# Moving one operand of the wide VectorE operations from SBUF to PSUM in a four-layer graph network

## The reference, cut to what matters

```python
x = layernorm(x + L0(x))   # two hops of a normalised, weighted neighbour sum, relu, times W0, plus b
x = layernorm(x + L1(x))   # attention, 8 heads of 32; the edge's term is relu(edge_attr3 @ encW + b)
x = layernorm(x + L2(x))   # attention, 8 heads of 32; the edge's term is edge_attr64 @ W_e @ attn_e
x = layernorm(x + L3(x))   # filter network on the edges, message x[col] * filt, sum by row, MLP, batch norm

# attention (L1 and L2 alike):
ex  = exp(alpha - segment_max(alpha, dst)[dst])
out = segment_sum(h[src] * ex / segment_sum(ex, dst)[dst], dst) + bias
# filter:
filt = silu(rbf @ Wf1 + bf1) @ Wf2 + bf2
agg  = segment_sum(x[col] * filt, row)
```

## Time and profile before

| | |
|---|---|
| median of 3 runs | 8960.01 us (8955.36 to 8965.5) |
| the profiled execution | 8954.23 us, span 8952.5 us |
| busy share of the span | PE 53%, DVE 70%, ACT 37%, POOL 62% |
| mean granted TensorE clock | 0.721 |
| attention 1 | about 2859 to 4010 us |
| nodes 1 | about 4030 to 4680 us |
| attention 2 | about 4695 to 5735 us |
| nodes 2 | about 5745 to 6335 us |
| filter | about 6340 to 7706 us |

### The profile page before, as it was taken

How to read it: one execution, slowest core, us unless ns; L and a number is a source line. 1 busy time by engine, 2 the same in 40 slices (tenths; PEclk the granted TensorE clock), 3 DMA queues, 4 the chain that set the end, 5 groups by cost and what they waited for, 6 DMA issues and landing times. The chain is left out here.

```text
span 8952.5 us, 103278 instructions
## 1 busy us (share of the span) xinstructions
PE 4724.6 (53%) x18908; PEld 3435.4 (38%) x18908; DVE 6238.9 (70%) x20123; ACT 3276.4 (37%) x8442; POOL 5545.9 (62%) x5121
## 2 busy tenths in 40 slices
PE   8855000019998333337771111100588888799944
PEld 4422000018886211225551111100455555688833
DVE  7899333348887999988987777799544444455577
ACT  4533001337776111117870000144322222244499
POOL 7877777765554666657767777677788888300000
PEclk9999555559998555559995555555677777899955
DMA  0299899989997444549994444599544444566699
GB/s 21 82 345 345 287 304 301 308 281 303 303 302 235 147 146 148 147 133 313 337 310 119 122 123 122 156 273 269 130 79 79 79 79 79 131 202 202 192 342 345
DMA packets 1143019, 1839.84 MB, mean 206 GB/s; under 512 B 218094, under 2 KB 564898, under 8 KB 1142374
## 3 DMA queue, kind: packets, MB, share of 16 engines
q1 hardware_dynamic: 637094, 927.78, 31.4%
q0 software_dynamic: 257536, 587.44, 25.7%
q10 hardware_dynamic: 247744, 318.00, 10.4%
HBM read 1044.55 MB, written 788.03 MB: 205 GB/s over the span
## 5 line engine op out<-in xcount | busy, mean ns | idle before, releaser
L701 POOL DMA_INDIRECT st<-S,last_i x1176 | 1421.0, 1208 | 650.3 <-issue 316.4
L915 POOL DMA_INDIRECT rows<-T,src_i x784 | 802.6, 1024 | 251.0 <-issue 248.6
L642 ACT ACTIVATE xo<-z,shift,rsd 128x256 f32<-128x256 f32 x1568 | 854.7, 597 | 4.4 <-issue 4.4
L1128 POOL DMA_INDIRECT A<-comb,ai x392 | 702.6, 1792 | 159.2 <-issue 143.9
L931 PE MATMUL psE<-encs,attr 4*128 4x256 f32 x784 | 404.8, 668 | 743.3 <-DMA attr<-in_attr3T 743.3
L946 ACT ACTIVATE ex<-diff 128x32 f32<-128x32 f32 x392 | 89.9, 229 | 1711.7 <-DVE diff L993 1711.7
L1200 DVE TENSOR_SCALAR eq<-psI,src_f 128x128 f32<-128x128 f32 x392 | 136.8, 349 | 742.6 <-DMA A<-comb,ai 708.7
L931 PE MATMUL psE<-fes,attr 64*128 64x8 f32 x784 | 199.5, 363 | 823.0 <-DMA attr<-in_attr64T 820.7
L477 DVE SCALAR_TENSOR_TENSOR sums<-sums,same,rows 128x256 f32<-128x256 f32 x784 | 380.7, 486 | 322.3 <-ACT rows L458 308.0
L1142 PE MATMUL psH<-rbf,wf1s 20*128 20x256 f32 x784 | 279.9, 486 | 600.2 <-DMA rbf<-in_rbfT 600.2
L931 PEld LDWEIGHTS psE<-encs,attr 4*128 4x128 f32 x784 | 227.4, 319 | 920.4 <-DMA attr<-in_attr3T 882.7
(11 more groups left out here) (232 smaller groups left out, 15603.8 us busy)
## 6 DMA issues: line engine op xcount, KB each, us to landing
X<-xo ACTq DMA_DIRECT2D x588, 256.0 KB
xt<-X SPq DMA_DIRECT2D x588, 256.0 KB
S<-sums SPq DMA_DIRECT2D x392, 272.0 KB, 2.4
A<-zero SPq DMA_DIRECT2D x392, 256.0 KB, 4.7
S<-sums SPq DMA_DIRECT2D x392, 256.0 KB, 4.1
xt<-in_x SPq DMA_DIRECT2D x392, 256.0 KB
T<-tt ACTq DMA_DIRECT2D x196, 280.0 KB
T<-tt ACTq DMA_DIRECT2D x196, 272.0 KB
```

The source lines that it names most:

```text
L642: ins = e.activation(y[s][:, k, :], z[s][:, k, :], ACT.Identity, bias=shift[s][:, k, :], scale=rsd[s][:, k, :])
L701: e.indirect_dma_start(st[s][:, k, :], None, sums_table, bass.IndirectOffsetOnAxis(ap=last_i[:, c:c + 1], axis=0))\
L915: e.indirect_dma_start(rows[s][:, k, :], None, table, bass.IndirectOffsetOnAxis(ap=src_i[:, c:c + 1], axis=0))\
L1128: e.indirect_dma_start(A[k], bass.IndirectOffsetOnAxis(ap=ai[s][:, k, :], axis=0), comb[s][:, k, :], None, compute_op=ALU.add).then_inc(si ...
```

## The change

In five stages one operand of each wide VectorE operation that had two SBUF inputs is placed in PSUM.

- **nodes 1 and 2**: the bias is copied once into the bank `psBias`; the denominators `den` lie in a bank `psDen`; `mix` writes its product into one of two banks `psMix` in place of `z`, and `add` reads it there. `mix` waits for the `add` of two steps back, and the wait for the old `z` moves to `add`.
- **attention 1 and 2**: the exponentials `ex` lie in two banks `psX`, so ScalarE's exponential waits for the `add` of two steps back where it waited for that of four steps back. The rescaled sum goes to a bank `psD` and is read there by the addition.
- **attention 1**: ScalarE rectifies in place in `psE`, and VectorE's product reads `psE` and still writes `enc`. TensorE's `encode` waits for `scored` of two steps back, where it waited for `rectified`.
- **filter**: the bias is added in place in `psF`, and the product reads `psF`.

No operation is added in a step and none is taken away; one copy of 128x256 is added ahead of each of the two node stages.

```diff
@@ layer_nodes @@
-                den = tiles("den", H) if layer else None
...
+                if layer:
+                    psBias, psDen, psMix = bank("psBias", D), bank("psDen", NS * G * H), [bank(f"psMix{j}", G * D) for j in range(2)]
+                    den = [psDen[:, s * G * H:(s + 1) * G * H].rearrange("p (g h) -> p g h", g=G) for s in range(NS)]
...
                         bias = (b0s, b1s, b2s)[layer]
+                        if layer:
+                            e.tensor_copy(psBias[:], bias[:]).then_inc(spread_bias, 1)
+                            e.wait_ge(spread_bias, 1)
+                            bias = psBias
...
-                                ins = e.tensor_scalar(den[s][:], v[:, :, :, HD], 1e-10, None, ALU.max)
+                                ins = e.tensor_scalar(den[s], v[:, :, :, HD], 1e-10, None, ALU.max)
...
-                            e.reciprocal(den[s][:], den[s][:]).then_inc(signal(st_["weighed"], s), 1)
+                            e.reciprocal(den[s], den[s]).then_inc(signal(st_["weighed"], s), 1)
...
-                            hold(e, *done(st_["normed"], i, s, NS))
+                            hold(e, *done(st_["summed"], i, s, 2))
                             v = st[s][:, :, 0:VW].rearrange("p g (h w) -> p g h w", h=H)
-                            e.tensor_tensor(z[s][:].rearrange("p g (h d) -> p g h d", h=H), v[:, :, :, 0:HD],
-                                            den[s][:].rearrange("p g (h w) -> p g h w", w=1).to_broadcast([P, G, H, HD]), ALU.mult)\
+                            e.tensor_tensor(psMix[s % 2][:].rearrange("p (g h d) -> p g h d", g=G, h=H), v[:, :, :, 0:HD],
+                                            den[s].rearrange("p g (h w) -> p g h w", w=1).to_broadcast([P, G, H, HD]), ALU.mult)\
                                 .then_inc(signal(st_["mixed"], s), 1)
...
+                                hold(e, *done(st_["normed"], i, s, NS))
                                 hold(e, *done(st_["mixed"], i, s))
-                                more = z[s][:]
+                                more = psMix[s % 2][:].rearrange("p (g d) -> p g d", g=G)
@@ attention_edges @@
+                psX = [ctx.enter_context(psum(f"psX{j}", [P, 512], F32)) for j in range(2)]
+                ex = [psX[s % 2][:, 0:G * 2 * H].rearrange("p (g h) -> p g h", g=G) for s in range(NS)]
+                psD = ctx.enter_context(psum("psD", [P, 512], F32))
...
-                            if layer == 1:
-                                hold(e, *done(rectified, i, s, 2))
-                            else:
-                                hold(e, *done(scored, i, s, 2))
+                            hold(e, *done(scored, i, s, 2))
...
-                            hold(e, *done(scored, i, s, NS))
-                            e.activation(enc[s][:].rearrange("p g d -> p (g d)"), psE[s % 2][:], ACT.Relu).then_inc(signal(rectified, s), 1)
+                            e.activation(psE[s % 2][:], psE[s % 2][:], ACT.Relu).then_inc(signal(rectified, s), 1)
...
-                            hold(e, *done(summed, i, s, NS))
-                            e.activation(ex[s][:], diff[s][:], ACT.Exp).then_inc(signal(exped, s), 1)
+                            hold(e, *done(summed, i, s, 2))
+                            e.activation(ex[s], diff[s][:], ACT.Exp).then_inc(signal(exped, s), 1)
...
-                                link(e.tensor_tensor(e4, e4, hd, ALU.mult))
+                                r4 = psE[s % 2][:].rearrange("p (g h d) -> p g h d", g=G, h=H)
+                                link(e.tensor_tensor(e4, r4, hd, ALU.mult))
...
-                                e.tensor_tensor(heads(sums[s][:, k, 0:VW]), heads(last), r, ALU.mult).then_inc(bsteps, 1)
+                                e.tensor_tensor(heads(psD[:, 0:VW]), heads(last), r, ALU.mult).then_inc(bsteps, 1)
                                 e.wait_ge(bsteps, i * (NS * B) + (s * B + n))
-                                ins = e.tensor_tensor(sums[s][:, k, 0:VW], sums[s][:, k, 0:VW], rows[s][:, k, 0:VW], ALU.add)
+                                ins = e.tensor_tensor(sums[s][:, k, 0:VW], psD[:, 0:VW], rows[s][:, k, 0:VW], ALU.add)
@@ filter_edges @@
-                            e.tensor_tensor(fl[s][:], psF[s % 2][:].rearrange("p (g d) -> p g d", g=G),
-                                            bf2s[:].rearrange("p (g d) -> p g d", g=1).to_broadcast([P, G, D]), ALU.add).then_inc(msteps, 1)
+                            filt = psF[s % 2][:].rearrange("p (g d) -> p g d", g=G)
+                            e.tensor_tensor(filt, filt, bf2s[:].rearrange("p (g d) -> p g d", g=1).to_broadcast([P, G, D]), ALU.add).then_inc(msteps, 1)
                             e.wait_ge(msteps, i * NS + (s + 1))
-                            e.tensor_tensor(fl[s][:], fl[s][:], rows[s][:], ALU.mult).then_inc(signal(message, s), 1)
+                            e.tensor_tensor(fl[s][:], filt, rows[s][:], ALU.mult).then_inc(signal(message, s), 1)
```

More of the change, by code:

```diff
@@ L673, in layer_nodes @@
                 stored_t = stage_of("stored_t", NS, 1 + layer % 2)
-                ones = semaphore("ones")
+                ones, spread_bias = semaphore("ones"), semaphore("spread_bias")
                 TURN, PRODUCT, ADD = 1, 2, 3 if layer == 0 else 1
@@ L879, in attention_edges @@
                 enc = tiles("enc", D) if layer == 1 else None
-                lg, dot, mp, diff, ex = tiles("lg", H), tiles("dot", H), tiles("mp", H), tiles("diff", 2 * H), tiles("ex", 2 * H)
+                lg, dot, mp, diff = tiles("lg", H), tiles("dot", H), tiles("mp", H), tiles("diff", 2 * H)
+                psX = [ctx.enter_context(psum(f"psX{j}", [P, 512], F32)) for j in range(2)]
+                ex = [psX[s % 2][:, 0:G * 2 * H].rearrange("p (g h) -> p g h", g=G) for s in range(NS)]
+                psD = ctx.enter_context(psum("psD", [P, 512], F32))
                 EW = D if layer == 1 else H
```

## The result

The changed kernel takes 8829.6 us in the median of 4 runs (8827.0 to 8831.6), the kernel before 8962.8 us in the median of its 4. The ratio is 0.9851, with a 95% interval of 0.984 to 0.9863. The two profiled executions are 8954.2 and 8827.0 us, 127 us apart. The forecast was 8840.

A forecast was written before the change was run, and what follows sets the result against it. GpSimd was taken to bound the filter and attention 2, VectorE nodes 2 and attention 1, the `psV` loop nodes 1. -71 - 36 - 8 - 5 + 0 = -120 us, from 8960 to 8840 us; range 8800 to 8925.

The forecast's parts named there:

- My 5 us for nodes 1: Nodes 1: GpSimd and VectorE get slack, the `psV` loop stays; step 3.25 to 3.22 us or so, -5 us.
- my idea of it: Gathers and scatters: GpSimd waits with reading row numbers until VectorE's second SBUF read is over; filter scatter 1.98 against 1.62 us.
- Filter -71: Filter: GpSimd sets the pace; the scatter of 1.98 us falls to 1.62, step 6.94 to 6.58 us, -71 us.
- attention 2 -36: Attention 2: GpSimd never rests; four gathers per step fall to 0.946 us each, step 5.18 to 5.0 us, -36 us.
- nodes 2 -8: Nodes 2: VectorE stays at 2.91 us per step, so only stalls go, 2.95 to 2.91, -8 us.
- attention 1's 0: Attention 1: GpSimd is not the limit in VectorE's chain, so shorter gathers give 0.
- what is late next: Attention 1: if a moved wait is not passed already, the `rectified` tile is late, 15 us per 1000 at stake.
- bounds of -25 and +74: VectorE's write to PSUM, in no row: cost bounded by -25 and +74 ns per operation, taken as 0.
- The rival's count of four operations in nodes 2: Dearer PSUM operands: L712, L736, L750, L763 each pay in nodes 2, six operations in attention 1; chance 0.16.
- one sign of being wrong: Signs against: L1008 or L1010 grow, a landing gap opens before the filter's first scatter, or its scatter stays at 1.98.
- The waits that the change moved: Waits of `mix`, `add`, the exponential and `encode`: each is passed already, cost 0.

The follow-up runs named there:

- two_sbuf_ahead: Changed kernel plus an unused 128x512 addition with two SBUF operands between the filter's two multiply operations; 8883.8 us in one run.
- one_sbuf_ahead: Changed kernel plus two unused 128x256 statistics operations, one SBUF operand each, between the filter's two multiply operations; 8845.1 us in one run.
- more_two_sbuf: Kernel before plus an unused 128x512 addition with two SBUF operands right behind the filter's product L1220; 8974.8 us in one run.

## Why the prediction was right

*Which engine sets each stage.* Right as far as the runs go. GpSimd in the filter and attention 2, VectorE in nodes 2, the loop through `psV` in nodes 1, VectorE's chain in attention 1. In nodes 1 the gathers are shorter by 23% (376 to 291 us of 500) and the stage by 0.4 us. That its loop through `psV` is the limit is read from the waits; no run changes that loop. My 5 us for nodes 1 were the difference of a mean and one pair of rows, and nothing stood behind them.

*A second SBUF read under way holds a gather or scatter back.* Right, and shown by the pair `two_sbuf_ahead` and `one_sbuf_ahead`: +0.27 us for a scatter, against nothing. One part of my idea of it, which the sum did not use, was wrong: back-to-back operations let GpSimd in between (`more_two_sbuf`). That is not always so. Of 34 gathers of the node stages before that began in the first of two such operations back to back, 11 waited until 0.557 us after the second one's start as well, and the longest gather took 1.957 us. What decides is open.

In the words of the Trainium skill, "SBUF — State Buffer", section "Who interferes with whom", a VectorE instruction with two SBUF inputs contends with a GpSimd instruction that reads SBUF. The trace agrees, 1.98 us against 1.59. The section's remark that `tensor_tensor` was not seen to stall DMA does not hold for these indirect DMAs, by the same two numbers.

*The sizes.* Filter -71 against -69, attention 2 -36 against -36, nodes 2 -8 against -8.5. That the whole fits as well as its parts (-120 against -123) is luck in part: attention 1 gave 9 us more than forecast, and nodes 1 nearly 5 less.

*The term that was mis-sized is attention 1's 0.* It is -9.2 us, -10.1 in the run with the attention stages alone, and -11.6 in the means of five executions. I had the row: the wait for the rectified tile, 15 us in 1000, and called it what is late next, never what might go. It fell to 5.5, and 9 us less per 1000 are about 11 over the stage's 1170. Which edit did it isn't told apart: ScalarE's two operations of a step became shorter with their output in PSUM (597 to 582 ns and 229 to 201), the in-place tile changed the waits of `encode`, and the gathers, which share the DMA engines with the load of `attr`, became shorter.

*The price of a PSUM operand on VectorE.* I took 0 with bounds of -25 and +74. Wide operations changed by -7 to +11 ns: in attention 1 the weighting of the rows 703 to 696, the rescaled sum (now from SBUF and PSUM into PSUM) 427 to 433, the addition 433 to 432; in nodes 2 `mix` 683 to 692; the filter's bias addition 684 to 695. The small ones of nodes 2 took more, the clamp (L731 before) 148 to 167 and the reciprocal (L736 before) 231 to 249. The rival's count of four operations in nodes 2 left out the clamp, which writes `psDen` too. The step of nodes 2, where each would have counted, went from 2.908 to 2.904 us in the median. By the letter one sign of being wrong came, the rescaled sum grew; but by 6 ns, and the median step of attention 1 is the same. "VectorE: DVE Perf Modes" of the Trainium skill, section on the TRN2 errata, has 62 cycles more for a source in PSUM. No row here shows them, in an isolated chain or back to back.

*The waits that the change moved* show up in no row of VectorE. In the two attention stages and the two node stages of the changed kernel it waits for what it waited for before, the rectified tile, ScalarE's `sd` and the gathered rows, and for 3 us of 850 for `psE` in attention 2, where `encode` waits as it did.

## What to carry to other kernels

When GpSimd issues indirect DMAs without a rest and they take longer than their minimum (here 945 ns), look at what VectorE runs when they start. If it is an operation with two SBUF inputs, one of them can be had from PSUM, for wide operations at a price of 11 ns or less here. The gain is the lengthening times the number of transfers, but only in stages where GpSimd sets the step; elsewhere it is what the late transfers stalled, 8 to 12 us a stage here, or nothing. Then look the other way for small VectorE operations that end exactly with a gather.

## What the runs showed of the hardware that I had not expected

A small VectorE operation from SBUF to SBUF (128x8, two of them per step) waited for the end of a gather under way, 0.24 us over its 0.23, and stopped doing so with its output in PSUM. That took 0.13 us off the median step and 12 to 19 us off the stage. ScalarE's exponential of 128x32 takes 201 ns into PSUM and 229 into SBUF. What waits for a scatter's landing begins 2.4 us after the scatter's end in both kernels, with scatters of 1.98 and 1.59 us. What a gather or scatter loses to an operation with two SBUF inputs is what is left of that operation's first 0.56 us (128x512) or 0.31 us (128x264) when it begins.
